# Centring rows on GpSimd and forming edge features in strided pieces, in a two-layer graph network kernel on one core

## What is computed

```python
edge_index = jnp.stack([src, dst])
h = jnp.maximum(_layernorm(x, axis=-1), 0.0)
x = x + _L0_gnn_ref(h, node_vec1, edge_attr_4, edge_attr_8, ...)
h = jnp.maximum(_layernorm(x, axis=-1), 0.0)
x = x + _L1_gnn_ref(h, edge_attr_4, ...)

# in _L0_gnn_ref
h = jax.nn.silu(edge_scalars @ fc_w1 * (1.0 / np.sqrt(8.0)))
weight = h @ fc_w2 * (1.0 / np.sqrt(64.0))       # (edges, 192): w1, w2 (64 each), w3, w4 (32 each)
m0a = gs * ys * w1_                               # gs, gv: linear map of the source row
m0b = jnp.sum(gv * yv[:, None, :], -1) * INV3 * w4_
m1a = gs[..., None] * yv[:, None, :] * w2_[..., None]
m1b = gv * ys[..., None] * w3_[..., None]
mid = segment_sum(concat(m0a, m0b, m1a, m1b), edge_dst) / sqrt(16)
return jnp.cos(angle) * scfeat + jnp.sin(angle) * conv
```

## Time and profile before

| what | value |
| --- | --- |
| median of 3 runs | 2483.28 us (2479.98 to 2484.08) |
| span of the profiled execution | 2863.6 us, 55863 instructions |
| PE busy | 1940.9 us, 68% |
| DVE busy | 1954.7 us, 68% |
| POOL busy | 1745.2 us, 61% |
| ACT busy | 1560.1 us, 54% |
| mean granted TensorE clock | 0.828 of full speed |

### The profile page before, as it was taken

The page is one execution under the profiler, slowest core; times in us unless marked ns, Lnnn a source line. Parts: engine busy times, 40 slices in busy tenths (PEclk is TensorE's granted clock), DMA queues, the critical chain, the costliest instruction groups (busy, mean ns, idle before and its releaser), DMA issues.

```text
span 2863.6 us, 55863 instructions
## 1 busy us (share of the span) xinstructions
PE 1940.9 (68%) x12874; PEld 1820.7 (64%) x12874; DVE 1954.7 (68%) x8628; ACT 1560.1 (54%) x4412; POOL 1745.2 (61%) x1676
## 2 busy tenths in 40 slices
PE   0888888878878888878883343434344777777877
PEld 0777777777877777777773333323233777767777
DVE  2889888887888888888884655556555444444444
ACT  0667677776777777777774444545453222222222
POOL 1656666665666666766656565655565666666665
PEclk9989999998999999999995555555555999999898
DMA  9444544443444444454543232323332333333332
GB/s 79 142 143 169 172 170 171 172 172 138 169 172 170 173 169 164 162 179 147 180 154 124 87 89 87 93 87 97 88 99 83 81 89 88 92 92 90 94 95 74
DMA packets 223602, 364.52 MB, mean 127 GB/s; under 512 B 115938, under 2 KB 133149, under 8 KB 223405
## 3 DMA queue, kind: packets, MB, share of 16 engines
q1 hardware_dynamic: 176524, 289.81, 32.1%
q0 software_dynamic: 47040, 74.31, 9.8%
HBM read 176.85 MB, written 194.78 MB: 130 GB/s over the span
## 4 chain that ended last, share of the span: by engine, by line
DVE 31%; PE 25%; issue 14%; another core or an unknown queue 11%; POOL 8%; ACT 6%; SPq 2%; DMA 1%; DVEq 1%; ACTq 0%; POOLq 0%
DVE st L1334 3%; PE bank L969 3%; PE bank L1154 3%; POOL x_e L581 3%; POOL inv L628 3%; DVE x L1353 2%; DVE su_e L1203 2%; PE bank L964 2%; PE bank L1166 2%; DVE st L1362 2%; PE bank L1163 2%; ACT h L755 2%; PE bank L1176 2%; DVE x L1599 2%
## 5 line engine op out<-in xcount | busy, mean ns | idle before, releaser
L628 POOL TENSOR_TENSOR inv<-var,minus_half 128x8 f32<-128x8 f32 x196 | 327.7, 1672 | 256.5 <-DVE var L1210 253.4
L625 POOL TENSOR_TENSOR yo<-x,h 128x640 f32<-128x640 f32 x196 | 305.8, 1560 | 147.8 <-ACT h L755 145.4
L969 PE MATMUL bank<-wp,hT 128*128 128x160 f32 x1568 | 392.6, 334 | 1.6 <-DVE x L1353 0.7
L755 ACT ACTIVATE h<-x,nmr,inv 128x160 f32<-128x160 f32 x784 | 342.2, 514 | 6.1 <-POOL nmr L642 6.1
L587 POOL DMA_INDIRECT h_all<-h,i_put x196 | 203.4, 1038 | 217.9 <-ACT h L871 146.0
L964 PE MATMUL bank<-ident,h_e 128*128 128x128 f32 x392 | 83.0, 350 | 358.9 <-ACT h_e L878 229.2
L587 POOL DMA_INDIRECT out<-yo,i_put x196 | 202.1, 1031 | 197.2 <-DVE feat L1706 63.8
L1353 DVE SCALAR_TENSOR_TENSOR x<-bank,scl,x_all 128x160 f32<-128x160 f32 x784 | 254.3, 372 | 89.1 <-PE bank L970 46.0
L969 PE MATMUL bank<-wp,eT 128*128 128x160 f32 x784 | 274.5, 444 | 54.5 <-ACT eR L886 27.3
L934 ACT ACTIVATE tot<-bank 128x160 f32<-128x160 f32 x196 | 59.6, 304 | 455.7 <-remote 207.1
L964 PEld LDWEIGHTS bank<-ident,h_e 128*128 128x128 f32 x392 | 57.5, 184 | 367.9 <-DVE hr_e L1215 244.1
(11 more groups left out here) (173 smaller groups left out, 6292.4 us busy)
## 6 DMA issues: line engine op xcount, KB each, us to landing
x_all<-in_xa SPq DMA_DIRECT2D x98, 644.0 KB, 5.8
h_all<-h SPq DMA_DIRECT2D x98, 640.0 KB, 2.9
out<-yo SPq DMA_DIRECT2D x98, 640.0 KB, 3.3
q_row<-row_tab SPq DMA_DIRECT2D x98, 256.0 KB
sum_tab<-tot SPq DMA_DIRECT2D x49, 322.0 KB, 4.2
y_tab<-yo SPq DMA_DIRECT2D x49, 320.0 KB
x<-y_tab SPq DMA_DIRECT2D x49, 320.0 KB
cv<-sum_tab SPq DMA_DIRECT2D x25, 322.0 KB
```

Of the source, the lines that this page charges most:

```text
L625: nc.gpsimd.tensor_tensor(yo[j][:, a:b], x1[j][:, a:b], h1[j][:, a:b], ALU.add).then_inc(d_y, 1)
L628: nc.gpsimd.tensor_tensor(inv[:, 0:n], var[:, 0:n], minus_half[:, 0:n], ALU.pow).then_inc(signal, 1)
L755: ins = nc.scalar.activation(h1[j][:, k * D:(k + 1) * D], x1[j][:, k * D:(k + 1) * D], ACT.Relu, bias=nmr2[j][:, k:k + 1], scale=inv2[j][: ...
L969: nc.tensor.matmul(dst_ps, main[:, t * P:(t + 1) * P], wp[:, w:w + D], start=True, stop=False)
```

## The change

Six things are done.

1. `bn_stats` takes two rows in one instruction, with their elements alternating: it keeps separate statistics of even and odd elements, so each half is one row's mean and sum of squares. The instructions halve in number and the joining instructions (`moment_part`) go. The temporaries su, df, sq, m2, neg, var go with them.
2. The mean is subtracted on POOL (`centre`: for a unit one instruction of 8 x 128 elements a partition and one of 8 x 32, for a quad 4 x 128 and 4 x 32) in place of ACT's relu instructions and DVE's `rest_of`. The relu is done by ACT while it copies the transposed block out of PSUM. In pass 2 the subtraction is on DVE (`p2_centre`).
3. The inverse root of units is ACT's `Sqrt` and DVE's `reciprocal` (`dense_root1`, `dense_root2`, `dense_inverse`, `dense_scale`, `dense_inverse2`, `dense_shift2`). A quad's root stays a `pow` on POOL.
4. The features that the edge vector enters are three `scalar_tensor_tensor` of 32 elements (stride 3 on one side, the weight in PSUM) with the vector's component as a scalar; the other 96 are one product. Formerly one instruction formed 192 products and another multiplied 96 of them by the vector.
5. The hidden layer of the edge network is computed for all quads ahead of pass 1: 13 groups of 4 quads, each a load, two products of 512 columns, two `Silu`, a store into hid_tab. Pass 1 loads 128 KB a quad.
6. POOL's order in pass 1 is `p1_gather` (w even), `dense_centre(w)`, `dense_y(w-3)`, then `p1_centre` and `p1_scale` (w odd). All the work on quads stands there.

```diff
+            def net_load(g):
+                n = min(GQ, Q - g * GQ)
+                wait(sp, n_mm, 2 * (g - 1))
+                sp.dma_start(n_sct[g % 2][:, 0:n * P]...).then_inc(n_in[g % 2], 16)
+            def net_store(g):
+                sp.wait_ge(n_act, 2 * g + 2)
+                sp.dma_start(hid_tab[g * GQ:g * GQ + n]...).then_inc(n_st[g % 2], 16)
+            for j in range(2):
+                sp.wait_ge(n_st[j], 16 * ((NB + 1 - j) // 2))
+            def p1_hidden(q):
+                wait(sp, e_pw, q.times(GQ, -GQ))
+                sp.dma_start(q_hid[j][:, :], hid_tab[q.times(1)]).then_inc(e_hid[j], 16)
...
-            def inverse_root(inv, var, n, signal):
-                nc.gpsimd.tensor_tensor(inv[:, 0:n], var[:, 0:n], minus_half[:, 0:n], ALU.pow).then_inc(signal, 1)
+            def centre(into, rest, rows, st, g, signal):
+                x = x3(rows, XW, g)
+                nc.gpsimd.tensor_tensor(x3(into, P, g), x[:, :, 32:D], bc_last(stat(st, g, 1), P), ALU.subtract)
+                nc.gpsimd.tensor_tensor(x3(rest, 32, g), x[:, :, 0:32], bc_last(stat(st, g, 1), 32),
+                                        ALU.subtract).then_inc(signal, 1)
+            def dense_centre(u):
+                pool.wait_ge(d_ln1, u.times(1, 1))
+                wait(pool, d_tr, u.times(2, -2))
+                centre(hb[u.mod(2)], hr[u.mod(2)], x_in[u.mod(4)], st1[u.mod(4)], GD, d_cen)
...
-            def dense_relu(u, h):
-                act.wait_ge(d_ln1, u.times(5, 3))
+            def root(into, st, n, signal):
+                nc.scalar.activation(into[:, 0:n], stat(st, n, 2), ACT.Sqrt, bias=eps[:, :], scale=1.0 / D).then_inc(signal, 1)
...
-                nc.scalar.activation(hT[h][:, :], bank[0][:, :], ACT.Copy)
+                nc.scalar.activation(hT[h][:, :], bank[0][:, :], ACT.Relu)
...
+            def paired_stats(st, pair, rows, width):
+                two_rows = rows[:, 2 * pair * width:(2 * pair + 2) * width].rearrange("p (g f) -> p f g", f=width)
+                return V.bn_stats(st[:, 2 * pair:2 * pair + 2, :].rearrange("p g k -> p (g k)"), two_rows[:, 0:D, :])
...
+            def dense_inverse2(u):
+                v.wait_ge(d_sq2, u.times(1, 1))
+                wait(v, d_h1, u.times(2, -2))
+                V.reciprocal(inv2[j][:, :], sd2[j][:, :]).then_inc(d_nmr, 1)
...
-                    V.tensor_tensor(f[:, 128:320]..., w[:, 128:192]..., g[:, DS:D]..., ALU.mult).then_inc(e_fm, 1)
+                    for c in range(3):
+                        V.scalar_tensor_tensor(f[:, 224 + c:320:3], w[:, 160:192], ed(j, t, 1 + c, 2 + c), g[:, DS + c:D:3],
+                                               ALU.mult, ALU.mult)
...
-                    v.wait_ge(e_fm, n.times(1, 1))
-                    V.tensor_tensor(f[:, 224:320]..., f[:, 224:320]..., bc_mid(ed(j, t, 1, 4), DU), ALU.mult).then_inc(e_ft, 1)
+                    V.tensor_tensor(f[:, 128:224]..., bc_last(w[:, 128:160], 3), g[:, DS:D]..., ALU.mult).then_inc(e_ft, 1)
```

More of the change, by code:

```diff
@@ L205, in gnn_kernel @@
         h_e = sb("h_e", [P, GQ * P])
-        hr_e = two("hr_e", [P, GQ * 32])
+        hr_e = sb("hr_e", [P, GQ * 32])
         part2 = two("part2", [P, GQ * D])
@@ L851, in step @@
                     dense_h1(u - 2, 1)
-            net_silu(At(0, 0, 2))
-            p1_relu(At(0, 0, 2))
+            for g in range(-(-Q // GQ)):
+                net_silu(g)
             p1_copy(At(0, 0, 2))
@@ L873, in p2_h1 @@
                 ins.then_inc(r_h1, 1)
-            def p2_relu(q):
-                act.wait_ge(r_ln1, q.times(5, 3))
-                for t in range(GQ):
-                    ins = nc.scalar.activation(h_e[:, t * P:(t + 1) * P], x_q[q.mod(4)][:, t * XW + 32:t * XW + D],
-                                               ACT.Relu, bias=neg_e[q.mod(2)][:, t:t + 1])
-                ins.then_inc(r_relu, 1)
             def p2_copy(q):
@@ L1093, in slot @@
                 if (s - 1).within(T):
-                    p1_feat_t(s - 1, q1 if u.mod(2) == 0 and h == 1 and q1.within(Q) else None)
+                    p1_feat_t(s - 1)
                 if (s - 2).within(T):
@@ L1102, in step @@
             def step(u):
-                q = At(u.i, u.c // 2, 2)
-                odd = u.mod(2) == 1
                 slot(u, 0)
-                if not odd and (q + 1).within(Q):
-                    net_mm(q + 1)
                 if u.within(U):
@@ L1114, in _ @@
             pe.wait_ge(e_z, 1)
-            net_mm(At(0, 0, 2))
+            for g in range(-(-Q // GQ)):
+                net_mm(g)
+            pe.wait_ge(n_act, 2 * -(-Q // GQ))
             p1_tr(At(0, 0, 2))
@@ L1379, in p1_stats @@
                 v.wait_ge(e_g[j], q.over(2, 64, 64))
-                for t in range(GQ):
-                    ins = V.bn_stats(st_e[j][:, t, :], x_e[j][:, t * XW:t * XW + D])
+                for pair in range(GQ // 2):
+                    ins = paired_stats(st_e[j], pair, x_e[j], XW)
                 ins.then_inc(e_ln, 1)
-            def p1_moments(q, part):
-                j = q.mod(2)
-                v.wait_ge(e_ln, q.times(5, part))
-                moment_part(part, st_e[j], su_e[j], df_e[j], sq_e[j], m2_e[j], neg_e[j], var_e[j], GQ, e_ln)
-            def p1_rest_rows(q):
-                rest_of(hr_e[q.mod(2)], x_e[q.mod(2)], neg_e[q.mod(2)], GQ, e_ln)
             def p1_selectors(q):
@@ L1439, in step @@
                 rows = u.mod(2) == 0 and q1.within(Q)
+                odd = u.mod(2) == 1 and q1.within(Q)
                 if now:
                     dense_x1(u - 1, 0)
+                if (u - 2).within(U):
+                    dense_inverse2(u - 2)
+                if now:
                     dense_x1(u - 1, 1)
+                if (u - 2).within(U):
+                    dense_shift2(u - 2)
+                if now:
                     dense_stats2(u - 1, 0)
@@ L1525, in p2_stats, with p2_centre @@
             def p2_stats(q):
+                j = q.mod(2)
                 v.wait_ge(r_g[q.mod(4)], q.over(4, 64, 64))
-                for t in range(GQ):
-                    ins = V.bn_stats(st_e[q.mod(2)][:, t, :], x_q[q.mod(4)][:, t * XW:t * XW + D])
+                for pair in range(GQ // 2):
+                    ins = paired_stats(st_e[j], pair, x_q[q.mod(4)], XW)
                 ins.then_inc(r_ln1, 1)
-            def p2_moments(q, part):
+            def p2_centre(q):
                 j = q.mod(2)
-                v.wait_ge(r_ln1, q.times(5, part))
-                moment_part(part, st_e[j], su_e[j], df_e[j], sq_e[j], m2_e[j], neg_e[j], var_e[j], GQ, r_ln1)
+                v.wait_ge(r_ln1, q.times(1, 1))
+                wait(v, r_tr, q.times(1))
+                x = x3(x_q[q.mod(4)], XW, GQ)
+                V.tensor_tensor(x3(h_e, P, GQ), x[:, :, 32:D], bc_last(stat(st_e[j], GQ, 1), P), ALU.subtract)
+                V.tensor_tensor(x3(hr_e, 32, GQ), x[:, :, 0:32], bc_last(stat(st_e[j], GQ, 1), 32),
+                                ALU.subtract).then_inc(r_cen, 1)
             def p2_angle(q, part):
@@ L1606, in p2_stats2 @@
                 v.wait_ge(r_x1, q.times(2, 2))
-                for t in range(GQ):
-                    ins = V.bn_stats(st2[j][:, t, :], x1[j][:, t * D:(t + 1) * D])
+                for pair in range(GQ // 2):
+                    ins = paired_stats(st2[j], pair, x1[j], D)
                 ins.then_inc(r_ln2, 1)
-            def p2_moments2(q, part):
-                j = q.mod(2)
-                v.wait_ge(r_ln2, q.times(4, part))
-                moment_part(part, st2[j], su2[j], df2[j], sq2[j], m22[j], neg2[j], var2[j], GQ, r_ln2)
             def p2_norm2(q, part):
@@ L1654, in p2_step @@
                 if a:
-                    rest_of(hr_e[q.mod(2)], x_q[q.mod(4)], neg_e[q.mod(2)], GQ, r_ln1)
                     p2_angle(q, 3)
@@ L1674, in p2_step @@
                     p2_angle(q, 7)
-                if b:
-                    for part in (1, 2, 3):
-                        p2_moments2(q - 1, part)
             v.wait_ge(d_y, 2 * U)
```

301 lines of the change are left out of this document (128 added, 173 removed).

## The result

The changed kernel takes 2525.9 us (median of 4, 2520.5 to 2528.79) against 2481.63 (2478.22 to 2484.08) for the kernel before, run on the same chip: ratio 1.0184, 95% interval 1.0164 to 1.0205. It is slower by 1.8%, where 2414, faster by 2.8%, was forecast. It lies inside the stated range of 2335 to 2530, near its slow end, and on the other side of no change. The profiled execution of the changed kernel has a span of 2518.7 us, in line with its median.

The account below looks back on a forecast made before the run. Pass 1 was taken as held by a dependency loop through POOL plus clock-lowering stalls. Pass 1 -103, prologue +48, pass 2 -25 made -80 us on 2863.6, factor 0.972, so 2414 us on the median; range 2335 to 2530.

Parts of the forecast that it names:

- 27.0 us a quad in place of 29.1: Pass 1: the quad shortens from the first profile's 29.1 us to 27.0, worth -103 us, between -200 and 0.
- that of pass 2: Pass 2: less work on ScalarE and DVE shortens the steps, worth -25 us out of 0 to 73 of gain.
- I take the same factor for it: Whole kernel: the profiled span's predicted factor of 0.972 also holds for the unprofiled median of 2483.28 us, giving 2414.
- the disturbances: Pass 1: DVE stalls behind POOL make features late, TensorE waits and its clock falls; 2.3 us a quad, 113 in all.
- a block of 15.8 us on POOL: Pass 1: POOL's stretch of work per quad between DVE's waits goes from 15.4 to 15.8 us after the change.
- The sign that the prediction named for its removal: Pass 1: TensorE's waits for DVE's features under 2 us and a clock above 0.95 would show the stalls had gone.
- Where DVE can now stall: Pass 1: DVE's scale of a unit may wait behind POOL's 1,024-element subtraction, 0 to 2.4 us, taken as 1.2 a step.
- the ring as drawn: Pass 1: a dependency loop through POOL's yo, roots, gathers and scale to DVE's x keeps a quad near 26 to 27 us.
- Prologue: Ahead of pass 1: 13 edge-network groups at 3.6 us each, with nothing beside them, add 48 us, between 30 and 65.
- Rival 1: Pass 1: features stay late and the clock falls as often, quad stays 29.1; 2503 us, slower; chance 0.27.
- Rival 2: Pass 1: POOL's subtractions cost more, its loop ends last and DVE's x waits for yo; 2601 us; chance 0.12.
- Rivals 3 and 4: Pass 1: TensorE alone bounds, quad 25 us, 2308 us, chance 0.14; alternating-row statistics run slower, over 2600 us, chance 0.05.

Follow-up runs that it names:

- experiment 5: The changed kernel with the two selector comparisons moved on DVE ahead of the outer product of the odd step's second slot: 2440.54 us, ratio 0.9837 to the kernel before.
- experiment 7: The kernel before with the two selector comparisons moved earlier on DVE, ahead of the features: 2554.91 us, ratio 1.0298 to the kernel before.
- experiment 6: The changed kernel with POOL waiting for the two selector comparisons before each even step's dense-row subtraction, DVE's order untouched: 2525.52 us, ratio 1.0187 to the kernel before.
- experiment 8: The changed kernel with the dense rows' 1024 columns centred on ScalarE instead of POOL: 2430.12 us, ratio 0.9803 to the kernel before.
- experiment 2: The kernel before with only the edge network of all tiles moved ahead of pass 1: 2529.97 us, ratio 1.0191 to the kernel before.
- experiment 3: The changed kernel with the edge network back in pass 1's loop, nothing else changed: 2476.52 us, ratio 0.9996 to the kernel before.

## Why the prediction was wrong

**The step that failed** is "I take 27.0 us a quad in place of 29.1 ... 49 x 2.1 = -103 us". The 27.0 was right (26.8). The 29.1 was a property of one execution, 15% longer than the median; the kernel before ordinarily runs at 27.1, so the term measured -18 us where -103 was put down. With the other terms as forecast, -18 makes +5 of the sum of -80. The second term that failed is that of pass 2: the time behind pass 1 grew by 7 us, where -25 was put down. The same fault sits in "I take the same factor for it": the disturbances were carried over to the median by a factor, though a median 380 us shorter can't hold them. The clean quads of 26.8 in the earlier trace rows were the better baseline, and 27.0 - 26.8 would have given +10 for pass 1, +33 in all with the other terms: 2516.

**The 27.0 was partly luck.** It rested on a block of 15.8 us on POOL, worked out from rates that were too high, and had no hold of `same` in it. Without that hold the quad is 25.0 (experiment 5), the lower end of the stated 25 to 29.1; the hold adds 1.7 us. The number was hit by errors that cancel.

**What a disturbance is.** The stall of DVE behind POOL's instruction, in the earlier trace rows, is real and ordinary (1305 ns again). That it costs 2.3 us a quad, through the clock, was wrong: clock 0.97 in the ordinary execution, 0.3 us a quad. The sign that the prediction named for its removal did come: TensorE's waits for the features are 0.7 us at most in the changed kernel, and the clock is 1.00. It was worth 0.3 us a quad. A dear fall of the clock behind such waits was seen, outside the first profile, only in experiment 7.

**Where DVE can now stall.** The scale was named, at 1.2 us; it stalls 0.4 (537 ns). The selector, not named, stalls 4.3. The error was to price a stall by one POOL instruction, as in the earlier trace rows. "DVE's saved time covers it" fell with it: DVE is busy 362 of 400 us against 361 before, and 302 in the same stretch of experiment 6, where `same` is not held: the saving is all spent in `same`.

**POOL.** Rates were estimated high: 1.92, 0.63, 1.05 and 0.41 us against 2.4, 0.74, 1.3 and 0.46. That a ring through it holds the quad near 26 to 27 was right as to the engines, but the ring as drawn lacked DVE's `same`: in the changed kernel POOL waits 6.3 us a quad for DVE, and DVE's x hardly ever for yo. The Trainium skill (GPSIMD Engine Reference, section 3, Performance versus the Vector engine) puts such work on VectorE. By its figure hb would be an estimated 2.25 us; it took 1.92. Moving hb away gave 96 us all the same (experiment 8), but to ScalarE; no run had it on VectorE.

The rule to weigh was another. By the earlier trace rows, DVE's su_e, with both inputs in SBUF, and neg_e waited for a running instruction of POOL, and the new code put four POOL instructions in a row beside `same`, which has both inputs in SBUF. The Trainium skill (SBUF — State Buffer, section Who interferes with whom) says that a DVE instruction with two SBUF inputs contends with a GpSimd instruction that reads SBUF, that the shared ports are an exclusive lock, and that the order of issue decides who blocks. The trace agrees on who is blocked, `same`, which started 0.80 us after hb; the block was longer than one instruction, 5.26 us over four.

**Features.** "Nothing, between -0.2 and +0.3 us a tile": measured alone +16 us in pass 1, 0.08 us a tile, within that range but not nothing.

**TensorE and ScalarE.** The "0.7 to 1.2 us" fewer on TensorE bought nothing (experiment 2). ScalarE's 7.8 us were too many: it is busy 309.5 of 400 us before and 247.4 after, 21.0 and 16.6 us a quad, 4.4 less; and giving back two table loads a quad cost nothing (experiment 3). Neither ended last in these two kernels.

**Prologue.** Right in size: +48 forecast, +49.8 read, 3.9 us a group against 3.6. The 3.6 was half of a round trip, with TensorE's 2.4 at the full clock below it; in the trace TensorE needs 3.6 us a group at the full clock and is the busy one, so the size was in part luck.

**Pass 2.** -25 forecast. By the scatters of h_all it takes 487.1 us before (1443.8 to 1930.9) and 499.7 after (1470.8 to 1970.5): +12.6, partly regained where pass 1 hands over. The step that failed is "POOL waited for ScalarE's h 97 of 400 us": that wait is in the first profile alone. Ordinarily POOL's DMAs follow each other at 0.3 us, before and after, from 1500 to 1900 us:

```profile
L587 POOL DMA_INDIRECT h_all<-h,i_put x154 | 156.5, 1016 | 47.0 <-issue 47.0
L581 POOL DMA_INDIRECT x_all<-in_xa,i_dst x153 | 151.3, 989 | 46.6 <-issue 46.6
```

```profile
L611 POOL DMA_INDIRECT h_all<-h,i_put x148 | 165.3, 1117 | 45.1 <-issue 45.1
L605 POOL DMA_INDIRECT x_all<-in_xa,i_dst x150 | 145.7, 972 | 45.7 <-issue 44.2 <-ACT h L895 1.5
```

Their busy and issue time fill the 400 us, so POOL bounds pass 2 and no work taken from ScalarE or DVE could shorten it. A step is 10.0 us before, not the 13.8 read from the long profile, and 0.26 longer after. The longer part is in the scatters: 1117 ns in place of 1016, in each step one that runs beside DVE's yo. The 37 such took 1.46 us in the mean, the other 111 took 1.00. One of them:

```profile
1701.63 0.82 DVE L1610 TENSOR_TENSOR yo<-x,h 128x640 f32<-128x640 f32 x1
1701.67 1.65 POOL L611 DMA_INDIRECT h_all<-h,i_put  x1 [0.30 <-issue]
```

That DVE's instruction lengthens the scatter is only read from the overlap, and overlap alone is not enough: three of the 37 took 0.98, and in the kernel before, where scatters ran beside yo too, 21 such took 1.05. Why they differ stays open. No run tested this part by itself.

**The rivals.** Rival 1's 2503 is nearest in microseconds, by a mechanism that isn't there (clock 1.00). Rival 2 looked at the right two engines, but its sign, DVE's x waiting for yo, is not there (4.0 us in 1000): POOL's instructions were fast, and it was DVE behind `same` for which POOL waited. Rivals 3 and 4 are refuted: 26.8 a quad, and 484 ns for a pair of rows against 311 for each before.
